# Permutation operands in six column sets and four row sets, ScalarE's columns one group further ahead

## What is computed

```
n_f  = layernorm(x)
feat = concat([n_f[edge_src], n_f[edge_dst]], axis=1)
e_hh = relu(feat[:128] @ W_hh + b_hh)            # the first edge tile
e_oo = relu(feat[128:768] @ W_oo + b_oo)         # the next five tiles
e_ho = relu(feat[768:] @ W_ho + b_ho)            # the other 58 tiles
logit = e_f @ W_a + b_a
alpha = softmax of logit over the edges of one destination
z_f   = segment_sum(alpha * n_f[edge_src], edge_dst)
h_new, o_new = relu(concat([n_f, z_f]) @ W_hn or W_on + bias)
x = x + concat([h_new, o_new])
x = x + ffn(layernorm(x))     # top 4 of 256 experts, silu, weighted sum
```

## Time and profile before

| | us |
|---|---|
| median of the runs | 730.29 (730.01 to 731.85) |
| the profiled execution | 730.32 |
| its span on the core | 728.0 |
| PE busy | 695.9 (96%) |
| DVE busy | 502.3 (69%) |
| ACT busy | 380.4 (52%) |
| POOL busy | 218.8 (30%) |

### The profile page before, as it was taken

One profiled execution on the slowest core, in us unless ns is written; L12 is line 12 of the kernel. 1 busy time (PEld: TensorE's weight loads), 2 busy tenths in 40 slices (PEclk: granted clock), 3 DMA queues, 4 the chain that ended last, 5 costly groups with the idle time before them and its releaser, 6 DMA issues.

```text
span 728.0 us, 9581 instructions
## 1 busy us (share of the span) xinstructions
PE 695.9 (96%) x3308; PEld 546.0 (75%) x3308; DVE 502.3 (69%) x705; ACT 380.4 (52%) x486; POOL 218.8 (30%) x338
## 2 busy tenths in 40 slices
PE   3999999899989899999999999999999999999998
PEld 2877877676555557677878888888888888888886
DVE  5997698498999998768889444564445645356453
ACT  3854889766765555547655343353433544335430
POOL 4073368798886887600500000000000000000000
PEclk9999999999999999999999999999999999999999
DMA  8975332433000004709545556544565444654411
GB/s 292 376 278 217 129 115 62 171 115 116 2 1 0 1 2 160 257 5 346 186 157 181 210 185 230 195 151 164 182 230 202 143 173 173 230 210 139 184 43 59
DMA packets 55179, 114.21 MB, mean 157 GB/s; under 512 B 2246, under 2 KB 35398, under 8 KB 55147
## 3 DMA queue, kind: packets, MB, share of 16 engines
q1 hardware_dynamic: 54538, 112.95, 43.3%
q0 software_dynamic: 160, 0.66, 0.3%
q10 hardware_dynamic: 448, 0.20, 0.1%
HBM read 112.74 MB, written 1.05 MB: 156 GB/s over the span
## 4 chain that ended last, share of the span: by engine, by line
PE 69%; POOL 14%; ACT 5%; DVE 5%; issue 5%; DMA 2%; DVEq 0%; SPq 0%; ACTq 0%; POOLq 0%
PE ps L1385 20%; PE ps L1387 19%; PE ps L1386 19%; POOL peak L557 5%; POOL pen L562 4%; POOL oh_src L559 4%; PE ps L1354 3%; PE ps L1618 2%; ACT chunk_col L683 2%; ACT chunk_gap L678 2%; POOL wlo L568 1%; DVE wlo L863 1%; PE ps L1698 1%; DMA raw<-in_L_gnn_W_on_dram 1%; PE ps L1375 1%
## 5 line engine op out<-in xcount | busy, mean ns | idle before, releaser
L863 DVE TENSOR_TENSOR wlo<-raw,whi 128x2048 fp32r<-128x2048 f32 x99 | 224.6, 2291 | 58.7 <-ACT whi L620 57.9
L620 ACT ACTIVATE whi<-raw 128x2048 fp32r<-128x2048 f32 x104 | 196.2, 1911 | 84.9 <-PE ps L1387 67.0
L1385 PE MATMUL ps<-whi,nT 128*128 128x512 f32 x392 | 157.7, 402 | 0.3 <-ACT act_g L819 0.3
L1387 PE MATMUL ps<-wlo,nT 128*128 128x512 f32 x392 | 153.6, 392 | 0.0
L1386 PE MATMUL ps<-whi,nT 128*128 128x512 f32 x392 | 153.4, 391 | 0.0
L1051 DVE SCALAR_TENSOR_TENSOR ps<-ps,xt 128x1024 f32<-128x1024 f32 x79 | 96.1, 1227 | 1.9 <-PE ps L1411 1.0
L1385 PE MATMUL ps<-whi,gT_hi 128*128 128x512 f32 x240 | 93.4, 389 | 0.0
L1387 PE MATMUL ps<-wlo,gT_hi 128*128 128x512 f32 x240 | 93.4, 389 | 0.0
L1386 PE MATMUL ps<-whi,gT_lo 128*128 128x512 f32 x240 | 93.4, 389 | 0.0
L1311 DVE TENSOR_TENSOR gw<-act_g,route 128x512 f32<-128x512 f32 x32 | 20.7, 690 | 105.2 <-ACT act_g L827 105.1
L1385 PEld LDWEIGHTS ps<-whi,nT 128*128 128x128 f32 x392 | 74.0, 189 | 18.7 <-issue 3.2
(11 more groups left out here) (270 smaller groups left out, 920.1 us busy)
## 6 DMA issues: line engine op xcount, KB each, us to landing
raw<-n_L_ffn_values_down_dram SPq DMA_DIRECT2D x16, 2048.0 KB, 8.4
raw<-in_L_ffn_values_up_dram SPq DMA_DIRECT2D x16, 2048.0 KB, 7.3
raw<-in_L_gnn_W_hh_dram SPq DMA_DIRECT2D x8, 1024.0 KB, 7.0
raw<-in_L_gnn_W_oo_dram SPq DMA_DIRECT2D x8, 1024.0 KB, 6.4
raw<-in_L_gnn_W_ho_dram SPq DMA_DIRECT2D x8, 1024.0 KB, 4.8
raw<-in_L_gnn_W_hn_dram SPq DMA_DIRECT2D x8, 1024.0 KB, 4.8
raw<-in_L_gnn_W_on_dram SPq DMA_DIRECT2D x8, 1024.0 KB, 6.2
xt<-in_x_dram SPq DMA_DIRECT2D x4, 512.0 KB, 7.1
```

Source lines behind the costliest of these rows:

```text
L620: nc.scalar.activation(half(whi, s, j, down), half(raw, s, j, down), ACT.Copy)\
L863: nc.vector.tensor_tensor(half(wlo, s, j, down), half(raw, s, j, down), half(whi, s, j, down).bitcast(F32), ALU.subtract)\
L1385: nc.tensor.matmul(o, a_hi, b_hi, start=start, stop=False)
L1387: return nc.tensor.matmul(o, a_hi, b_lo, start=False, stop=stop)
```

## The change

Columns get six sets, rows four. The columns' sets don't lie in a tensor of their own any more but in `nf` (the normed nodes, free between the first transposes and the window stage), so that the listing names `nf` where ScalarE and GpSimd write columns. The writer of group n waits for group n - 6 (columns) or n - 4 (rows). ScalarE's queue has the columns of group 3 directly behind those of group 2, ahead of `table_hi(1, 1)`, and from there on each group of columns stands one place earlier. VectorE's queue has the rows of groups 10 and 11 ahead of `lo(1, 4)`, those of 12 between its halves, 13 and 14 behind it, and then both halves of `lo(0, 5)`.

```diff
--- before.py
+++ after.py
@@ -60,6 +60,8 @@
 CHUNK = 4
 REGS = 8
 EARLY = 3
+ROW_SETS = 4
+COL_SETS = 6
 ROW = 80
 CHUNKS = (JT + CHUNK - 1) // CHUNK
 
@@ -143,8 +145,7 @@
         with ExitStack() as first:
             ohx = sb("ohx", [P, 2, 8, P], F32R, first)
             idx_b = sb("idx_b", [P, 2, HEAD * P], I32, first)
-            chunk_row = sb("chunk_row", [P, 2, CHUNK, P], F16, first)
-            chunk_col = sb("chunk_col", [P, 2, CHUNK, 2 * WN], F16, first)
+            chunk_row = sb("chunk_row", [P, ROW_SETS, CHUNK, P], F16, first)
         with ExitStack() as routing:
             sim = sb("sim", [P, NT, XP], F32, routing)
             rtmp = sb("rtmp", [P, 2, XP], F32, routing)
@@ -178,6 +179,8 @@
             part_idx = sb("part_idx", [P, 2, WN], F16, edge)
             head_gap = sb("head_gap", [P, 4, P], F16, edge)
         fold = nf[:, 0, :]
+        chunk_col = nf[:].rearrange("p t n -> p (t n)").bitcast(F16)[:, 0:COL_SETS * CHUNK * 2 * WN]\
+            .rearrange("p (s j n) -> p s j n", s=COL_SETS, j=CHUNK)
         node_first = nf[:].rearrange("p t n -> p (t n)").bitcast(BF16).rearrange("p (w e) -> p w e", e=P)
         node_last = raw[:, 1, 0:D].bitcast(BF16).rearrange("p (w e) -> p w e", e=P)
 
@@ -544,10 +547,10 @@
             head_destinations(2)
             pool.wait_ge(sorted_ready, 1)
             for n in range(CHUNKS):
-                if n >= 2:
-                    pool.wait_ge(permuted, n - 1)
+                if n >= COL_SETS:
+                    pool.wait_ge(permuted, n - COL_SETS + 1)
                 for j in range(CHUNK * n, min(CHUNK * n + CHUNK, JT)):
-                    last = nc.gpsimd.tensor_scalar(chunk_col[:, n % 2, j % CHUNK, 0:WN], iota16[:, 0:WN], keep[:, 2, j:j + 1],
+                    last = nc.gpsimd.tensor_scalar(chunk_col[:, n % COL_SETS, j % CHUNK, 0:WN], iota16[:, 0:WN], keep[:, 2, j:j + 1],
                                                    keep[:, 0, j:j + 1], ALU.is_equal, ALU.mult)
                 last.then_inc(srccol_ready, 1)
 
@@ -669,8 +672,8 @@
             def destination_columns(n):
 
                 act.wait_ge(sorted_ready, 1)
-                if n >= 2:
-                    act.wait_ge(permuted, n - 1)
+                if n >= COL_SETS:
+                    act.wait_ge(permuted, n - COL_SETS + 1)
                 first, count = CHUNK * n, min(CHUNK, JT - CHUNK * n)
                 if n:
                     act.wait_ge(dstcol_ready, n)
@@ -680,7 +683,7 @@
                 last.then_inc(far_ready, 1)
                 act.wait_ge(far_ready, n + 1)
                 for j in range(first, first + count):
-                    last = nc.scalar.activation(chunk_col[:, n % 2, j % CHUNK, WN:2 * WN], chunk_gap[:, j % CHUNK, :],
+                    last = nc.scalar.activation(chunk_col[:, n % COL_SETS, j % CHUNK, WN:2 * WN], chunk_gap[:, j % CHUNK, :],
                                                 ACT.Relu, bias=keep[:, 1, j:j + 1], scale=keep[:, 4, j:j + 1])
                 last.then_inc(dstcol_ready, 1)
 
@@ -708,15 +711,15 @@
             hi(1, 3)
             hi(0, 4, parts=(0,))
             destination_columns(2)
+            destination_columns(3)
             hi(0, 4, parts=(1,))
             table_hi(1, 1)
-            destination_columns(3)
+            destination_columns(4)
             late_destinations(3)
-            destination_columns(4)
+            destination_columns(5)
             late_destinations(4)
-            destination_columns(5)
+            destination_columns(6)
             late_destinations(5)
-            destination_columns(6)
             destination_columns(7)
             destination_columns(8)
             hi(1, 4, parts=(0,))
@@ -1002,10 +1005,10 @@
             def chunk_rows(n):
 
                 dve.wait_ge(sorted_ready, 1)
-                if n >= 2:
-                    dve.wait_ge(permuted, n - 1)
+                if n >= ROW_SETS:
+                    dve.wait_ge(permuted, n - ROW_SETS + 1)
                 for j in range(CHUNK * n, min(CHUNK * n + CHUNK, JT)):
-                    last = nc.vector.tensor_scalar(chunk_row[:, n % 2, j % CHUNK, :], iota16[:, 0:P], keep[:, 3, j:j + 1],
+                    last = nc.vector.tensor_scalar(chunk_row[:, n % ROW_SETS, j % CHUNK, :], iota16[:, 0:P], keep[:, 3, j:j + 1],
                                                    None, ALU.is_equal)
                 last.then_inc(row_ready, 1)
 
@@ -1093,15 +1096,14 @@
                 if 3 < i + 3 < HEAD:
                     head_onehot(i + 3)
                 chunk_rows(i + 4)
+            chunk_rows(10)
+            chunk_rows(11)
             lo(1, 4, parts=(0,))
-            chunk_rows(10)
+            chunk_rows(12)
             lo(1, 4, parts=(1,))
-            chunk_rows(11)
-            lo(0, 5, parts=(0,))
-            chunk_rows(12)
-            lo(0, 5, parts=(1,))
             chunk_rows(13)
             chunk_rows(14)
+            lo(0, 5)
             decode()
             table_lo(2, 0)
             lo(1, 5)
@@ -1451,8 +1453,8 @@
                 pe.wait_ge(srccol_ready, n + 1)
                 pe.wait_ge(dstcol_ready, n + 1)
                 for j in range(CHUNK * n, min(CHUNK * n + CHUNK, JT)):
-                    last = nc.tensor.matmul(bank(3 if n < EARLY else 6)[:, 0:2 * WN], chunk_row[:, n % 2, j % CHUNK, :],
-                                            chunk_col[:, n % 2, j % CHUNK, :], start=j in (0, EARLY * CHUNK),
+                    last = nc.tensor.matmul(bank(3 if n < EARLY else 6)[:, 0:2 * WN], chunk_row[:, n % ROW_SETS, j % CHUNK, :],
+                                            chunk_col[:, n % COL_SETS, j % CHUNK, :], start=j in (0, EARLY * CHUNK),
                                             stop=j in (EARLY * CHUNK - 1, JT - 1))
                 last.then_inc(permuted, 1)
```

## The result

The changed kernel takes 727.64 us (median, 725.3 to 729.4), the kernel before 730.32 us in the runs beside it (728.49 to 733.1). The ratio of the runs is 0.9956, with a 95% interval of 0.9945 to 0.9967: 3.2 us less, 2.4 to 4.0. (It isn't the quotient of the two medians, which is 0.9963, or 2.7 us less; both lie within the interval.) Forecast were 727.1 us and 3.2 us less. The span of the profiled execution is 725.2 us instead of 728.0.

The account below looks back on a forecast made before the run. ScalarE's queue was taken to bound the permutation, with TensorE waiting 3.9 us ahead of its matmuls. Ending it 3.2 us earlier, nothing added or given back, gave 730.3 - 3.2 = 727.1 us; range 725.0 to 729.6.

Parts of the forecast that it names:

- ScalarE's queue bounds the permutation: Permutation: ScalarE's late queue is the one cause behind all 3.9 us of TensorE's waits there, including those put down to VectorE.
- The slot is free, the queue 2.70 us shorter: ScalarE: idle 1.45 and 1.16 us pay for group 3's earlier columns; from group 7 on, columns come 2.70 us earlier.
- The heads: TensorE: waits of groups 3 to 6 go; the fifth head waits for VectorE's product, group 7 comes 0.9 us earlier.
- Group 13: Permutation on TensorE, four-tile groups 0 to 14: this one comes at 134.6 us, waiting 1.0, 3.2 us earlier than 137.82.
- VectorE pays nothing for GpSimd's earlier work: Column writing: GpSimd's 16 earlier instructions were taken to cost VectorE nothing.
- The rival with 10.3 us: 74 to 85 us: GpSimd's 16 instructions hold VectorE up 10.3 us, 5.5 reach the heads: 732.6 us; chance 0.04.
- The fall of the clock stays, and costs 1.6 us: Second tables on TensorE: the clock's fall between 146 and 150 us is kept at its price, 1.6 us of matmul time.
- My rival that it goes with the waits: Second tables: without groups 12 and 13's waits the clock may stay up, another 1.6 us go: 725.5 us; chance 0.13.
- Nothing given back downstream: Behind the permutation: an earlier end moves everything later, so the whole 3.2 us reach the end, span 724.8 us.

Follow-up runs that it names:

- e1: The changed kernel with ScalarE's order of before, deeper sets and VectorE's new order kept: 730.51 us, ratio 1.001 to the kernel before.
- e2: The changed kernel with VectorE's order of before, deeper sets and ScalarE's new order kept: 727.94 us, ratio 0.9969 to the kernel before.
- e4: The kernel before with six column sets and four row sets, both queue orders as before: 731.14 us, ratio 1.0019 to the kernel before.
- e6: The changed kernel with destination columns of groups 12 to 14 made by GpSimd instead of ScalarE: 726.49 us, ratio 0.9937 to the kernel before.
- e10: The kernel before with six column and four row sets, both old orders, run once more for its trace: 734.79 us.
- e8: The changed kernel with table 2's eight bias matmuls in two blocks of four: 726.58 us, ratio 0.9943 to the kernel before.
- e3: The changed kernel with four column sets instead of six and two row sets instead of four: 726.29 us, ratio 0.9952 to the kernel before.
- e9: The changed kernel with table 2's bias matmuls in two blocks and GpSimd making destination columns of groups 12 to 14: 725.46 us, ratio 0.993 to before.
- e7: The changed kernel with both tables' bias matmuls spread in pairs and GpSimd making destination columns of groups 12 to 14: 726.82 us, ratio 0.9944 to before.

## Why the prediction was right, and where it wasn't

*ScalarE's queue bounds the permutation.* Right. e1 takes the gain away, e2 leaves it but for 0.4 us, e4 shows that the sets alone give nothing.

*The slot is free, the queue 2.70 us shorter.* Right. The first table piece wasn't even 0.2 us late. Group 7's columns were forecast at 109.34 and start at 109.08, which is 2.80 us earlier than the 112.04 of before once 0.16 is taken off. The end of group 13's columns, forecast 134.55, is 134.27 (134.43 with the 0.16).

*The heads.* Forecast was a gain of 0.9 us and no wait ahead of groups 3 to 6; measured are 0.74 (115.12 + 0.16 against 116.02), with a wait of 0.23 ahead of group 5. I had left VectorE's rows of group 5 out: they stand behind head 4's one-hots and were late by that much as soon as ScalarE wasn't. The wait ahead of head 5 is 0.32 where I said 0.9: that sum took the gain of the start for the wait, and group 5's wait had made group 6 later. This miss cost nothing, and not by luck: without a further wait group 13 would have come at 133.63 (130.54 + 3.09), and its columns came only at 134.27. The prediction's list of waits also left one out, 0.65 us ahead of group 10 in the trace of before; it went with the others:

```profile
126.08 0.42 PE L1454 MATMUL ps<-chunk_col,chunk_row 128*128 128x148 f16 x4 [0.65 <-ACT chunk_col L683]
```

*Group 13.* Forecast 134.6, measured 134.41 (134.57 with the 0.16). Its wait reads 0.63, I forecast 1.0. By starts it is 134.41 - (130.54 + 3.09) = 0.78; the idle time in brackets begins only at the modelled end of the matmul before, so it is the smaller. The forecast of 1.0 was a distance of starts and is 0.2 too large.

*VectorE pays nothing for GpSimd's earlier work.* Nearly. Beside 36 pieces in a row the two subtractions took 4.55 us instead of 4.49, the eight one-hots 1.80 instead of 1.67 and the rows behind them 0.88 instead of 0.80. The idle time behind these went from 4.87 to 4.57 us, that is 0.3 us of cost, all covered. The rival with 10.3 us is refuted. GpSimd paid more: its last two pieces here, beside the subtractions at 119.38 and 122.23, took 3.57 us, and those of e6's group 13 7.19 us for four. The exclusive lock that the Trainium skill names ("SBUF — State Buffer", "SBUF: two separate sides") agrees with the long pieces; on VectorE it shows little in these traces.

*The fall of the clock stays, and costs 1.6 us.* Right in both for the profiled execution. It came again behind the bias matmuls; by the mean grants 5 of 18 executions were without it. Its price in the tables is 1.53 us by e1, 1.63 by e10 (table 1 with and without it), and 1.15 plus the 0.4 of one block by e8. My rival that it goes with the waits is refuted: e6 has no wait ahead of groups 12 and 13 and still has the fall (slots to first product 32.08). The page of the Trainium skill "TensorE: Matmul & The Clock Gate", section "Part 1: The HAM clock gate", ties the low level to an idle array. That doesn't explain the falls in the tables: TensorE was busy throughout the 4 us ahead of them (4.00 us from 138 to 142 in the changed kernel, and from 68 to 72 in e1). What stood there were matmuls over 5 rows. All eight profiles with these in one block have the fall in table 2, and none of the four with them parted has it. That the parting keeps the clock up each time isn't shown, nor why it does.

*Nothing given back downstream.* Here a step failed by its size: 3.5 us at the window stage are 2.8 in the span (3.3 and 2.6 once the 0.16 is taken off), since the load at 329 us took 7.77 instead of 7.04 us. In the twelve profiles it takes 6.60 to 8.18, with no order by kernel (e4 7.19, its second execution 8.18). That speaks for chance and against the change as the cause; with one or two profiles of each kernel it isn't proved. I had taken the later part as TensorE's alone; one load there is on the path, and it belongs into the range. The sort's end too moves from execution to execution (63.85 to 64.94 us in kernels other than e1, e4 and e10), by the load of W_hh where that is on the chain. How much of the spread of the runs the two make up isn't shown. So that the ratio gives just the 3.2 us forecast, where this trace's span gives 2.8, is in part luck; what bears the prediction out are the times of its steps.

## What to carry to other kernels

Where an engine waits for a late piece, follow the piece's own queue back: the largest waits bore VectorE's name, and ScalarE's order cured them. Deeper buffers pay only where a queue's order is changed to use them; here two sets more of one operand sufficed, and of the other none. Before removing a cause of throttling count what the removal adds: eight bias matmuls spread in pairs cost 1.2 us a table, most of the fall's 1.5, and were spread in a table that had no fall too; in two blocks, in one table, they cost 0.4.

## What the runs showed of the hardware

Matmuls that contract over 5 rows were followed by a grant of 0.50 for some 3 us though TensorE was busy throughout: in table 2 of before, changed, e1, e2, e3, e4, e6 and e10, and in table 1 of e1 and e10 alone. A block of such matmuls among full ones adds about 0.4 us, by starts of 0.32 to 0.34 us instead of 0.23 on going over to the other kind and behind the first of it.

The clock also fell within VectorE's window stage, with no such matmul ahead: in e9 at 214 to 218 us, in e7 at 238 to 244, in e1 at 244 to 248. There TensorE had just waited. In e7:

```profile
238.40 0.49 PE L1413 MATMUL ps<-tab_src,ring 128*128 x1 [1.63 <-DVE ps L1056]
```

Two waits of 1.60 to 1.78 us stand in this stage of every profile, near these places. In e9, e7 and e1 one of the two was followed by a fall, in all other cases none was. The falls cost nothing there: from the first to the last window product are 100.19, 100.47 and 100.49 us in e9, e7 and e1, and 100.41 in the changed kernel without a fall. So the falls of the tables and those of this stage stand behind different work, and matmuls over 5 rows aren't the clock's only occasion to fall.
